# Transformer block on eight cores: token loads issued from GpSimd instead of ScalarE, and the entry of the last feed-forward product waiting chunk by chunk

## The reference, cut to what matters

```python
xn = _layernorm(x, axis=-1)
x = x + attn(xn, Wqkv, bqkv, Wproj, bproj) + ffn(xn, w1, w2, h1, h2, w3)

def ffn(x, ...):                       # _tlin(x, w, s) = (x @ w.T) * s
    h = silu(_tlin(x, w1_w, w1_s)) * _tlin(x, w2_w, w2_s)      # 1024 -> 4096
    h = gelu(_tlin(h, h1_w, h1_s))                             # 4096 -> 4096
    h = gelu(_tlin(h, h2_w, h2_s))                             # 4096 -> 4096
    return _tlin(h, w3_w, w3_s)                                # 4096 -> 1024
```

## Time and profile before

| | us |
|---|---|
| timed runs, both | 6083.91 and 6726.84 |
| their median | 6405.38 |
| the profiled execution | 5844.48 |
| span in its profile, slowest core (core 7) | 5842.6 |
| spans of the eight cores in it | 5818.8 to 5842.6 |
| TensorE matmul busy | 5535.4 (95%) |
| VectorE busy | 1130.0 (19%) |
| ScalarE busy | 1164.7 (20%) |
| GpSimd busy | 131.1 (2%) |

### The profile page before, as it was taken

One profiled execution on the slowest core, in us unless ns is written; L12 is line 12 of the kernel. 1 busy time (PEld: TensorE's weight loads), 2 busy tenths in 40 slices (PEclk: granted clock), 3 DMA queues, 4 the chain that ended last, 5 costly groups with the idle time before them and its releaser, 6 DMA issues.

```text
span 5842.6 us, 71560 instructions; the slowest of 8 cores (5818.8 to 5842.6 us)
## 1 busy us (share of the span) xinstructions
PE 5535.4 (95%) x26368; PEld 2496.4 (43%) x26368; DVE 1130.0 (19%) x3360; ACT 1164.7 (20%) x2177; POOL 131.1 (2%) x255
## 2 busy tenths in 40 slices
PE   4786788999999999999999999999999999999999
PEld 2332333444444444444444444444444444444444
DVE  2240001241023300242002510124102330024100
ACT  0141000241003310042001511024100331014100
POOL 0000000000000000000000000000000000000000
PEclk9898889999999999999999999999999999999999
DMA  8999998434344343434434343443434334443443
GB/s 172 209 219 221 219 216 227 170 130 176 146 157 159 138 177 148 169 134 159 166 137 173 145 173 144 159 159 135 180 147 169 145 144 170 150 159 145 158 158 116
DMA packets 88161, 961.00 MB, mean 164 GB/s; under 512 B 8512, under 2 KB 8592, under 8 KB 29072
## 3 DMA queue, kind: packets, MB, share of 16 engines
q0 software_dynamic: 33600, 454.14, 28.0%
q1 hardware_dynamic: 32976, 451.95, 20.3%
q10 hardware_dynamic: 21248, 50.33, 2.5%
HBM read 939.61 MB, written 117.44 MB: 181 GB/s over the span
## 4 chain that ended last, share of the span: by engine, by line
PE 85%; DMA 13%; issue 1%; DVE 1%; ACT 1%; DVEq 0%; ACTq 0%; POOLq 0%; SPq 0%
PE PSF L234 77%; PE PSF L230 5%; DMA wbuf<-h 5%; DMA h_bf<-wbuf 3%; DMA xt<-x 3%; DMA wbuf<-w 2%; PE PSF L388 2%; PE PSB L472 0%; PE PSB L313 0%; PE PSF L384 0%; ACT L280 0%; PE PSB L474 0%; DVE Ao L512 0%; DVE stats L265 0%; DVE stats L267 0%
## 5 line engine op out<-in xcount | busy, mean ns | idle before, releaser
L234 PE MATMUL PSF<-Ar,wbuf 128*128 128x512 bf16 x9920 | 2220.2, 382 | 114.1 <-ACT Br L636 65.0
L234 PE MATMUL PSF<-Br,wbuf 128*128 128x512 bf16 x7936 | 1780.1, 383 | 50.0 <-DMA wbuf<-h 50.0
L234 PEld LDWEIGHTS PSF<-Ar,wbuf 128*128 128x128 bf16 x9920 | 963.3, 98 | 1285.9 <-issue 161.1
L234 PEld LDWEIGHTS PSF<-Br,wbuf 128*128 128x128 bf16 x7936 | 781.7, 99 | 1008.9 <-issue 90.7
L234 PE MATMUL PSF<-xn_f,wbuf 128*128 128x512 bf16 x4480 | 1082.6, 382 | 50.7 <-DMA wbuf<-w 49.7
L234 PEld LDWEIGHTS PSF<-xn_f,wbuf 128*128 128x128 bf16 x4480 | 440.4, 98 | 588.4 <-issue 67.2
L699 ACT ACTIVATE Ar<-PSF,v_h2s 128x512 bf16<-128x512 f32 x256 | 176.0, 687 | 1792.5 <-PE PSF L230 1792.5
L720 DVE SCALAR_TENSOR_TENSOR sum_f<-PSF,v_w3s,sum_f 128x512 f32<-128x512 f32 x64 | 48.1, 751 | 2267.8 <-PE PSF L230 2267.8
L570 DVE SCALAR_TENSOR_TENSOR Ar<-PSF,v_w2s,t 128x512 bf16<-128x512 f32 x256 | 192.3, 751 | 753.8 <-PE PSF L230 753.8
L550 ACT ACTIVATE t<-PSF,v_w1s 128x512 bf16<-128x512 f32 x256 | 175.1, 687 | 682.5 <-PE PSF L230 682.4
L636 ACT ACTIVATE Br<-PSF,v_h1s 128x512 bf16<-128x512 f32 x256 | 175.0, 687 | 570.0 <-PE PSF L230 568.2
(11 more groups left out here) (67 smaller groups left out, 1762.0 us busy)
## 6 DMA issues: line engine op xcount, KB each, us to landing
wbuf<-h_bf POOLq DMA_DIRECT2D x112, 2048.0 KB, 8.1
wbuf<-h_bf SPq DMA_DIRECT2D x112, 2048.0 KB, 7.9
wbuf<-w_bf POOLq DMA_DIRECT2D x42, 2048.0 KB, 8.0
wbuf<-w_bf SPq DMA_DIRECT2D x42, 2048.0 KB, 7.8
wbuf<-h POOLq DMA_DIRECT2D x32, 2048.0 KB, 31.3
h_bf<-wbuf SPq DMA_DIRECT2D x32, 2048.0 KB, 26.2
wbuf<-w POOLq DMA_DIRECT2D x12, 2048.0 KB, 31.8
w_bf<-wbuf SPq DMA_DIRECT2D x12, 2048.0 KB, 19.9
```

Of the source, the lines that this page charges most:

```text
L234: return lambda e: e.matmul(out=out, lhsT=lhsT, rhs=rhs, start=start, stop=stop, tile_position=tile_position)
```

## The change

Two edits. The load of x in `phase_L_pre_group` is put in GpSimd's list instead of ScalarE's, with the same wait ahead of it. And H2's Gelus record their marks, which W3's first group uses as one wait ahead of each of its 32 matmuls, in place of one wait for the last Gelu.

```diff
@@ phase_L_pre_group
                 a = xls[slot].inc(16)
-                E.add("scalar", WM(("xt", slot)),
+                E.add("gpsimd", WM(("xt", slot)),
                       lambda e, a=a, t=t, g=g, slot=slot: a(e.dma_start(
@@ phase_H
             O, K, OU = WSPECS[wname]
+            hmarks = []
...
                     bank_mark[b] = (as_, as_.n)
+                    hmarks.append((as_, as_.n))
                 unit_consumed[iu] = ts.n
-            return ts.n, as_.n
-
-        def phase_W3(t, src_ready):
+            return ts.n, as_.n, hmarks
+
+        def phase_W3(t, src_ready, src_chunk_marks=None):
...
                     waits = [W(*wval)] if jj == 0 else []
+                    kcw = None
                     if j == 0 and jj == 0:
-                        waits.append(W(src_ready[0], src_ready[1]))
+                        if src_chunk_marks is not None:
+                            kcw = [W(src_chunk_marks[kc][0], src_chunk_marks[kc][1])
+                                   for kc in range(K // P)]
+                        else:
+                            waits.append(W(src_ready[0], src_ready[1]))
                     waits.append(WB(b))
                     mmv = mm_group(slot, jj, K, OU, PSF[:, b, 0:T],
-                                   [Ar[:, kc, 0:T] for kc in range(K // P)], waits)
+                                   [Ar[:, kc, 0:T] for kc in range(K // P)], waits,
+                                   kc_waits=kcw)
@@ the loop over t
-            h2_mm, h2_ev = phase_H(t, "h2", "h2s", Br, Ar, (as_, h1_ev), (ts, h1_mm),
-                                   src_chunk_marks=gelu_marks)
+            h2_mm, h2_ev, h2_marks = phase_H(t, "h2", "h2s", Br, Ar, (as_, h1_ev),
+                                             (ts, h1_mm), src_chunk_marks=gelu_marks)
...
-            w3_mm_prev, sum_done = phase_W3(t, (as_, h2_ev))
+            w3_mm_prev, sum_done = phase_W3(t, (as_, h2_ev),
+                                            src_chunk_marks=h2_marks)
```

## The result

| | before | after |
|---|---|---|
| the execution profiled, us | 5844.48 | 5805.6 |
| its span, slowest core | 5842.6 (core 7) | 5804.0 (core 6) |
| median of the timed runs compared | 5845.6 | 5806.0 |
| ratio, 95% interval | | 0.9929 [0.9915, 0.9943] |

The change took about 39 us, 0.7%: within 2%, but far outside the scatter of the compared runs, which agree within 3 us for the kernel after and 10 us for the kernel before. The 6405.38 us ahead of the prediction was the median of two executions of 6083.91 and 6726.84 us, and in every execution that long whose cores are on record the cores of one die, or of both, show a lower granted clock: such dies, and two executions of the kernel after of 13,194 and 23,769 us that nothing here explains, are left out of every comparison here. So 5812 is to be held against 5806, and 32 us of forecast gain against 39.

What follows compares the result with a forecast made beforehand. It took tile 0 as bound by the DMA engines and tiles 1 to 7 by TensorE. From the profiled execution, 5844.5 - 9 - 4 - 10.8 - 8.3 = 5812.4 us; range 5800 to 6410.

Steps and rivals of the forecast that it cites:

- Sum: Subtracted four gains from the profiled 5844.5 us to get 5812.4; on the 6405.38 median the same 32 us would give 6373.
- How the numbers follow: Set chances and range: forecast 50%, own range 5806 to 5818, with most rivals to 5849, stretched to 6410 for the median.
- The start (term 9): Kernel start: x on GpSimd lets TensorE start at 37.7 us, 16.4 earlier; gain between 7 and 14, taken as 9.
- The rival in which the later weight loads carry through: Start gains nothing: weight loads 12.7 us later, carried to tile 0's end; 5838 us, chance 20%.
- the slower rival: Start: each x load on GpSimd's queue takes 15.1 us to land, weights start 23.5 us late; 5849 us, chance 8%.
- x in tile 0's H1 (term 4): Tile 0's H1: 54.2 us of Gelu waits go, but DMA engines are full; gain 0 to 5.4, taken as 4.
- the 5762 rival: Tile 0: its stalls come back in full, TensorE's idle time sets the pace and 54.2 us go; 5762 us, chance 8%.
- x in tiles 1 to 7 (term 10.8): Tiles 1 to 7, where TensorE is the path: six waits for H1's Gelu go, gaining their full 10.8 us.
- W3's entry (term 8.3): Entry from h2 into W3: 1.19 us lost in each of seven tiles is regained, 8.3 us; the 32 waits cost nothing.
- x's move brings nothing: Moved loads: x still comes late behind a casting load, ScalarE blocks as before, only W3's gain stays; 5836 us, chance 6%.
- W3's gain fails: W3's first group: per-chunk waits slow it or the gap shows up elsewhere; 5821 us, chance 8%.

Runs made afterwards that it cites:

- x_start: Kernel before with only tile 0's own four x loads on GpSimd's list: mean span 9.0 us less, ratio 0.9997 [0.9959, 1.0035].
- The better start: Kernel after with tile 0's first two x loads issued first in ScalarE's list: mean span 8.9 us less than kernel after, ratio to before 0.9918.
- x_later: Kernel before with only the x loads for tiles 1 to 7 on GpSimd's list: mean span 15.1 us less, ratio 0.9966.
- scalar_early: Kernel before with x loads of tiles 1 to 7 still on ScalarE, issued 4 to 6 groups earlier: mean span 15.4 us less, ratio 0.9971.
- w3_only: Kernel before with only W3's first group waiting chunk by chunk, x loads unmoved: mean span 13.4 us less, ratio 0.9976.
- w3_tile0: Kernel before with W3's chunk waits in tile 0 only: mean span 4.0 us more than before, 1.7 more without one die.
- before_again: Kernel before, unchanged, traced on chip B as reference: tiles 1 to 7 in 4837.2 us, mean over its cores.
- after_third: Kernel after, unchanged, run on chip C: mean span 5793.9 us, 34.7 less than before.
- tile0_stall: Kernel after with the four x loads issued in tile 0's H1 back on ScalarE, chip A: mean span 35.2 us less than before, ratio 0.9939.
- stall_again: Kernel after with the x loads issued in tile 0's H1 back on ScalarE, chip C: mean span 5792.8 us, 35.8 less than before.

## Why the prediction was right or wrong

**The number against its footing.** The working is for the profiled execution, and there 5812 stands 6 us above the 5806 measured. But beside a median of 6405.38 the same number reads as a change of 9%, and the range reached up to 6410 to cover it. The step that failed is this footing, in "Sum" and in "How the numbers follow", where a median of unknown make was allowed to stand for the kernel before. The runs compared put that kernel at 5845.6 us, on the level of the profiled execution, and the change at 39 us, 0.7%, not 9%. The trace of 5844.48 was the only execution whose parts could be read, so both the number and the range should have been tied to it: its own 5806 to 5849 was the informative range, and the 5806.0 measured stand at its lower edge. That 32 us came so near to 39 is partly luck: the terms below were off by 4 us one way and by some 11 the other. The statement that runs can tell only about 2% from no change was also too coarse: the compared runs resolve 0.15%, and the direction, faster, was clear.

**The start (term 9).** Right, in its range of 7 to 14. Step by step: first matmul forecast at 37.7, found at 39.49; weights at 24.0, found at 24.82; the fourth load free near 49, found at 52.03. Alone it gave 9.0 +- 1.7 us, or 10.5 without one die. The rival in which the later weight loads carry through is excluded by x_start, and the slower rival by the landing: statistics of group 0 started 5.0 us after the issue. The better start confirms the mechanism a second time.

**x in tile 0's H1 (term 4).** The direction of the argument was right, the size was not: in the kernel after it is worth nothing. (From the kernel before, with its late start, x_later and scalar_early each left 3 us for tile 0, on a split good to 2; so a small worth there is not excluded.) With full DMA engines, 52 us of TensorE's waiting changed its name and not the time. The missing share of 0.03 that I turned into 5.4 us is no loss of work: in that window the engines moved 221 GB/s, more than the 218 before it, and I had this number in hand, against the 5762 rival, but did not hold it against my own 4.

**x in tiles 1 to 7 (term 10.8).** Mechanism right, size too small: this is the term of the sum that was mis-sized most. Core 7 lost 24.9 us there, of which 8.3 are W3's; 16.6 are left for a term of 10.8. I counted the waits and not what follows them, which I had put at nothing without a reason. The longest had the price beside it, in the very row quoted: TensorE waits 2.99 us, and its next 31 matmuls take 9.74 us instead of 6.85. The windows of the kernel before show why:

```profile
1355.00:1365.00 10.00, 7.30 (x34) 3.14 (x32) 2.31 (x4) 3.60 (x5) 0.53 (x1) 0.97 0.37 143
1365.00:1368.00 3.00, 2.70 (x7) 1.02 (x8) 0.00 (x0) 0.73 (x2) 0.00 (x0) 0.50 1.05 273
1368.00:1371.00 3.00, 3.00 (x9) 1.03 (x7) 0.00 (x0) 0.00 (x0) 0.00 (x0) 0.50 0.79 311
...
1375.00:1382.00 7.00, 7.00 (x35) 3.13 (x32) 1.49 (x3) 1.78 (x2) 0.00 (x0) 1.00 0.22 75
```

After the wait the granted clock is 0.50, that is 1.2 GHz, for some 6 us, and then full again. The wait of tile 4 did the same; a wait of 1.55 us did not (timeline of the kernel before, core 7, and in the last row core 6):

```profile
2017.09 6.85 PE L234 MATMUL PSF<-Ar,wbuf 128*128 128x512 bf16 x31 [1.55 <-ACT Br L636]
...
3398.25 8.54 PE L234 MATMUL PSF<-Ar,wbuf 128*128 128x512 bf16 x31 [2.15 <-ACT Br L636]
...
3379.15 6.85 PE L234 MATMUL PSF<-Ar,wbuf 128*128 128x512 bf16 x31 [2.15 <-ACT Br L636]
```

The last row shows that the length of the wait alone does not decide: on core 6 of the same execution the same 2.15 us cost nothing more. In the five traces of kernels with these waits in tiles 1 to 7 (before, twice, w3_only, x_start, w3_tile0) no wait for the Gelu of H1 under 1.96 us was followed by the lower clock, and of the 62 longer ones 35 were and 27 were not, up to one of 3.18 us. What decides between them is not shown.

The sum for core 7: waits 10.8, lower clock 2.89 + 1.69 = 4.6, and 0.16 us beside each of the six waits, as 1.19 stood beside 1.04 in W3, 1.0: together 16.4 against 16.6. Because the lower clock hit core 7 twice, it was also the slowest core before; over all cores the loads were worth 12.3 us. There the same sum, from the trace before_again, is 10.1 us of waits, 1.0 beside them and 1.3 of lower clock (six falls on eight cores): it comes out too. The Trainium skill (TensorE: Matmul & The Clock Gate, Part 1) says that the array's clock is gated to half or full rate by how busy the engine has lately been; the trace agrees with the two rates, 0.50 behind the wait and 1.00 after it.

**W3's entry (term 8.3).** Right: 8.1 us by its own kernel, nothing in tile 0, and nothing for the waits themselves.

**What is left.** 9 + 0 + 16.4 + 8.3 = 33.7 of 38.6 us. The missing 5 us are tile 0's, which shortened by 13.8 us on the slowest core and by about 15 in the mean on chip B. On chips A and C, mean span less tiles 1 to 7 gives 14 to 15 us for after_third, tile0_stall and stall_again as well, so they repeat and are hardly a drift from one execution to the next. In mean spans the single edits add up to more than the whole (37.5 against 35.5), with the 5 us among them that w3_only brought in tile 0 and the same edit in tile 0 alone did not. What those 5 us are stays open.

Of the rivals, *x's move brings nothing* and *W3's gain fails* are excluded by single-edit kernels, the full return of the stalls by stall_again.

## What to carry to other kernels

Ask of each transfer where its issue stands in its engine's list, and what the wait behind it holds up; the queue itself made no difference here. A wait removed from an engine is worth its time only where that engine is the bound: the same stall was worth nothing in a stage whose DMA engines were full, and in a stage bound by TensorE it was worth its own length and a fifth (mean of all cores) to a half (core 7) more, once the clock behind it is counted. Tie a forecast to an execution that the trace shows, and keep a time of unknown footing out of its range.

## What the runs showed of the hardware

- A wait of TensorE of 2 to 3.5 us, in a stretch of otherwise full work, was followed by a granted clock of 0.50 in 35 of 62 cases (8.54 or 9.74 us for 31 matmuls instead of 6.85 on core 7); of 179 shorter waits above 0.8 us, none was.
- 8512 more waits on semaphores already fulfilled made tiles 1 to 7 0.3 us longer in all.
- In tile 0 with its casting loads, x stood in GpSimd's queue behind weights, so that its landing took up to 39.9 us after issue. It harmed nothing, for it was issued early: TensorE waited for no Gelu of H1. GpSimd itself waited eight times, 49.8 us in all, for the normalisation ahead of an x load, 11.7 of them at the start, and in tiles 1 to 7 TensorE waited for no weight load (kernel after, core 6):

```profile
POOL xt L255 <- DVE xn_tm L291: 49.8, 8, 9.6
```
